# Starting eight expert tiles while the last batches are still routed

## The reference, cut to what matters

```
x = x + attention(layernorm(x))          # linear attention with a 5-tap convolution of v, gated
x = x + moe(layernorm(x))                # 8 experts, the 2 best of each token
moe: p = softmax(y @ gate_w.T); for each token the two experts with the largest p
     h = silu(y @ w1[e] + b1[e]);  out += p[e] * (h @ w2[e] + b2[e])     # 128 -> 512 -> 128
```

## Time and profile before

| | us |
|---|---|
| median of 3 runs | 636.82 |
| the runs | 631.85 to 644.96 |
| the profiled execution, own time | 633.09 |
| its span, first to last instruction | 631.3 |
| PE busy | 538.6 (85%) |
| DVE busy | 464.5 (74%) |
| POOL busy | 373.4 (59%) |
| ACT busy | 295.6 (47%) |
| mean granted TensorE clock | 0.919 of 2.4 GHz |

### The profile page before, as it was taken

How to read it: one execution, slowest core, us unless ns; L and a number is a source line. 1 busy time by engine, 2 the same in 40 slices (tenths; PEclk the granted TensorE clock), 3 DMA queues, 4 the chain that set the end, 5 groups by cost and what they waited for, 6 DMA issues and landing times.

```text
span 631.3 us, 10741 instructions
## 1 busy us (share of the span) xinstructions
PE 538.6 (85%) x2977; PEld 430.6 (68%) x2977; DVE 464.5 (74%) x1391; ACT 295.6 (47%) x658; POOL 373.4 (59%) x318
## 2 busy tenths in 40 slices
PE   3999999999999999996302999999899999999970
PEld 2787777777877777775202888877677777877750
DVE  6567868888788888865451888886887788878860
ACT  2434423333233333312301677765776676767750
POOL 3333266677666777766760000178848888888885
PEclk9899979999899999985555999999999999999995
DMA  8415787775767741111138476788889999999844
GB/s 294 130 66 160 291 284 250 261 255 186 261 232 261 262 158 34 36 37 35 50 138 290 159 263 238 256 267 264 249 280 300 279 275 304 306 288 309 276 123 97
DMA packets 66827, 134.23 MB, mean 213 GB/s; under 512 B 8144, under 2 KB 26704, under 8 KB 61648
## 3 DMA queue, kind: packets, MB, share of 16 engines
q1 hardware_dynamic: 51408, 116.23, 52.1%
q0 software_dynamic: 15360, 17.32, 12.5%
HBM read 29.83 MB, written 62.54 MB: 146 GB/s over the span
## 4 chain that ended last, share of the span: by engine, by line
PE 63%; DVE 10%; issue 10%; POOL 5%; DMA 5%; ACT 2%; SPq 2%; POOLq 1%; another core or an unknown queue 1%; DVEq 0%; ACTq 0%
PE conv L419 5%; PE qp L483 5%; PE qp L421 4%; PE qp L482 4%; PE qp L419 4%; PE conv L420 4%; PE conv L421 4%; PE rows L414 4%; PE qp L420 4%; POOL xres L759 3%; PE kv L443 3%; PE kvp L419 3%; PE kvp L421 3%; PE kvp L420 3%; PE gate_wo L471 2%
## 5 line engine op out<-in xcount | busy, mean ns | idle before, releaser
L718 POOL DMA_INDIRECT rows_in<-yrow,slots x128 | 124.4, 972 | 55.4 <-issue 35.0
L755 POOL DMA_INDIRECT got<-rows_out,slots x64 | 68.0, 1062 | 102.8 <-issue 102.5
L759 POOL DMA_INDIRECT xres<-rows_out,slots x64 | 103.2, 1612 | 19.5 <-issue 19.2
L1065 DVE TENSOR_TENSOR hl<-hf,hh 128x512 fp32r<-128x512 f32 x156 | 108.8, 698 | 5.4
L1063 DVE CAST hh<-hf 128x512 fp32r<-128x512 f32 x156 | 71.4, 458 | 37.2 <-ACT hf L688 33.1
L688 ACT ACTIVATE hf<-qp,wst 128x512 f32<-128x512 f32 x104 | 72.3, 695 | 47.7 <-PE qp L421 31.9
L613 ACT ACTIVATE yrow<-xres,nb,rs 128x128 f32<-128x128 f32 x64 | 26.4, 482 | 54.1 <-DVE nb L933 49.7
L688 ACT ACTIVATE hf<-kvp,wst 128x512 f32<-128x512 f32 x52 | 36.1, 695 | 26.9 <-PE kvp L421 13.3
L419 PE MATMUL qp<-xT_h,wst 128*128 128x512 f32 x104 | 45.6, 438 | 2.0 <-DVE xT_l L1033 1.6
L740 POOL TENSOR_TENSOR rs<-ve,half 128x8 f32<-128x8 f32 x20 | 35.9, 1795 | 18.6 <-DVE ve L810 17.2
L674 ACT ACTIVATE yo<-gate_wo,wv 128x128 f32<-128x128 f32 x156 | 44.2, 373 | 0.9 <-PE gate_wo L414 0.7
(11 more groups left out here) (182 smaller groups left out, 1480.3 us busy)
## 6 DMA issues: line engine op xcount, KB each, us to landing
wst<-wres SPq DMA_DIRECT2D x39, 1030.5 KB
rows_out<-tail SPq DMA_DIRECT2D x28, 1280.0 KB
xg<-rows_in SPq DMA_DIRECT2D x39, 272.0 KB
rows_out<-yo SPq DMA_DIRECT2D x39, 256.0 KB
wraw<-in_w_experts SPq DMA_DIRECT2D x8, 512.0 KB, 4.2
out_x<-xres SPq DMA_DIRECT2D x16, 256.0 KB
rows_in<-tail SPq DMA_DIRECT2D x9, 272.0 KB, 4.2
rows_in<-yrow,slots POOLq DMA_INDIRECT x128
```

Of the source, the lines that this page charges most:

```text
L718: nc.gpsimd.indirect_dma_start(rows_in, bass.IndirectOffsetOnAxis(ap=slots[:, f, k, j:j + 1], axis=0), rows_of(f)[:, j, :], None).then_inc ...
L755: nc.gpsimd.indirect_dma_start(got[b % N_GOT][:, j, :], None, rows_out, bass.IndirectOffsetOnAxis(ap=slots[:, b, 1, j:j + 1], axis=0)).the ...
L759: nc.gpsimd.indirect_dma_start(xres[:, b * SUB + j, :], None, rows_out, bass.IndirectOffsetOnAxis(ap=slots[:, b, 0, j:j + 1], axis=0), com ...
L1065: nc.vector.tensor_tensor(hl[c][:], hf[c][:], hh[c][:].bitcast(F32), ALU.subtract).then_inc(s["h_low"], 1)
```

## The change

The expert stage no longer waits for the last batches. Names are those of the changed kernel.

- **Early table.** After eight batches (EARLY_FROM = 8) there are at least eight full pages (N_EARLY = 8). In steps 13, 14 and 15 of the attention stage PE and DVE build a small table of the eight full pages that were touched first (`trow_e`, `texp_e`), each part at the end of the DVE's step. It uses free columns of the PSUM bank of `kv`, so PE's `kv` matmuls of steps 14, 15 and 16 wait for the DVE's part before them.
- **Early start.** The attention loop ends after step 16 (NB + 1). SP loads the weights and rows of tile 0 once the attention's last uses of that memory are past, and PE starts tile 0 after `oT` of the last batch. DVE first finishes the choice of batch 13.
- **Drain in pieces.** What steps 17 to 20 and the table did is cut up and stands in `drain(t, c)` behind chunk c of tile t, on PE, ACT and DVE, from tile 0 to tile 5. ACT's exponentials of batches 14 and 15 stand between silus.
- **Table and tails.** SP writes the zero rows behind the lists ahead of its work for tile 6 (LAST_LOAD: before it loads the rows of tile 7 and the weights of tile 6), and waits for the full table and all scatters ahead of its work for tile 7 (TABLE_AT).
- **The way back.** `got` is now the memory of `yrow`, of which there are five instead of six, so N_GOT is 5: gather(b) waits for the add of batch b-5. A batch is added behind the tile of this rule: at least max(2(b+1)+7, 16) + 6, and at most one batch a tile. That gives tiles 22, 23, 24, 25, 26, 27, 28, 29, 31, 33 and so on to 45 for batches 0, 1, 2 ... 15.
- **Buffers.** The tiles' transposes have a PSUM bank of their own (XT), the banks of the `down` sums go from three to two, `xT_h` and `xT_l` from three to two, `hf`, `hh` and `hl` from four to three. The constants are loaded in two more transfers.

```diff
-N_GOT = 4
-LEAD, LAG = 2, 5
-N_YROW = 6
+N_H = DOWN_LAG + 1
+N_XT = 2
+LEAD = 2
+N_YROW = 5
+N_GOT = N_YROW
+N_EARLY = E
+EARLY_FROM = -(-(E * (TS - 1) + (N_EARLY - 1) * TS + 1) // (TOP_K * S))
+LAST_LOAD, TABLE_AT = N_EARLY - 2, N_EARLY - 1
...
+        got = [r[:, :, 0:D] for r in yrow]
...
-        HB, YB, TY = [qp[:, 0:512], qp[:, 512:1024], kvp[:, 0:512]], [kvp[:, 512:1024], KV[:], CV[:]], GW
+        HB, YB, TY, XT = [qp[:, 0:512], qp[:, 512:1024], kvp[:, 0:512]], [kvp[:, 512:1024], KV[:]], GW, CV
...
         def tiles_until(b):
-            return min(TOP_K * (b + 1) + E - 1, N_TILES)
+            return min(max(TOP_K * (b + 1) + E - 1, N_EARLY + E), N_TILES)
+        add_at = []
+        for b in range(NB):
+            add_at.append(max([tiles_until(b) + ADD_LAG + 1] + [t + 1 for t in add_at[-1:]]))
+        def added(t):
+            return add_at.index(t) if t in add_at else None
...
         @block.sync
...
-            sp.wait_ge(s["fill_ready"], 1)
-            for e in range(E):
-                r = sp.value_load(fill_at[0:1, e:e + 1], min_val=e * CAP, max_val=e * CAP + N_TOK)
-                sp.dma_start(rows_in[bass.ds(r, TS), :].rearrange("(p j) w -> p j w", p=P), tail[:]).then_inc(s["tails_in"], 16)
-            sp.wait_ge(s["table_ready"], 3)
+            def fill_ends():      # the same wait and loop
...
+            sp.wait_ge(s["clear_in"], N_CLEAR * 16)
+            sp.wait_ge(s["table_e"], 2)
+            scattered(EARLY_FROM)
+            for name in ("conv_psum", "k_sin", "vtok_ready", "ks_masked", "q_rot"):
+                sp.wait_ge(s[name], NB)
             load_weights(0)
...
             load_rows(0)
             for t in range(LAST_STEP + 1):
+                if t == LAST_LOAD:
+                    fill_ends()
+                if t == TABLE_AT:
+                    sp.wait_ge(s["table_ready"], 3)
+                    sp.wait_ge(s["tails_in"], E * 16)
+                    sp.wait_ge(s["dummy_in"], 16)
+                    scattered(NB)
                 if real(t + 1):
                     load_rows(t + 1)
                 if real(t) and t > 0:
                     load_weights(t)
...
         @block.tensor, step(i, par)
+                    after(pe, "touch_e", 1 if i == NB - 2 else 0)
+                    after(pe, "pos_e", 1 if i == NB - 1 else 0)
+                    after(pe, "table_e", 2 if i == NB else 0)
                     for j in range(SUB):
                         last = nc.tensor.matmul(KV[:, 0:D + 1], ktok[:, j, :], vtok[:, j, :],
...
-            for i in range(-LEAD, NB + LAG):
+            for i in range(-LEAD, NB + 1):
                 step(i, i % 2)
+            def drain(t, c):
+                if (t, c) == (0, 0):
+                    rank(NB - 3)
+                if (t, c) == (0, 2):
+                    leave_attention(NB - 1)
+                if (t, c) == (0, 3):
+                    rows_to_gate(NB - 2)
+                if (t, c) == (1, 0):
+                    gate(NB - 2)
+                if (t, c) == (2, 0):
+                    rank(NB - 2)
+                if (t, c) == (2, 3):
+                    rows_to_gate(NB - 1)
+                if (t, c) == (3, 0):
+                    gate(NB - 1)
+                if (t, c) == (4, 0):
+                    rank(NB - 1)
+                if (t, c) == (4, 2):
...                                        # slots_ready 16, then the matmul for cum_psum
+                if (t, c) == (5, 0):
...                                        # diag_ready, then two matmuls for touch_psum
+                if (t, c) == (5, 2):
...                                        # pick_ready, need_ready, then two matmuls for table_psum
-            pe.wait_ge(s["table_ready"], 3)
+            pe.wait_ge(s["o_ready"], NB)
             rows_to_features(0)
...
         @block.scalar
+            def drain(t, c):               # called behind chunk c, but not in chunk 2
+                if (t, c) == (0, 1):
+                    rows_normal(NB - 2)
+                if (t, c) == (0, 3):
+                    save_rows(NB - 2)
+                if (t, c) == (1, 0):
+                    save_logits(NB - 2)
+                if (t, c) == (1, 1):
+                    exponents(NB - 2)
...                                        # the same for NB - 1 at (2, 1), (2, 3), (3, 0), (3, 1)
         @block.gpsimd, gather(b)
+                if b < N_GOT:
+                    after(pool, f"scat{b}", fills(NB - 1 - b, N_YROW) * (SUB * TOP_K * 16), alone=True)
                 after(pool, "combined", b - N_GOT + 1, alone=True)
...
         @block.vector
+            def early_table(i):            # at the end of step(i)
+                if i == NB - 3:
...
+                    counts(early[:, 0:EARLY_FROM * E].rearrange("p (b e) -> p b e", b=EARLY_FROM), EARLY_FROM)
+                    link(nc.vector.tensor_scalar(valid[:], cum[:, EARLY_FROM - 1:EARLY_FROM], entry_from, float(TS),
+                                                 ALU.subtract, ALU.is_ge))
+                    link(nc.vector.tensor_tensor(n_touched[:], n_touched[:], valid[:], ALU.mult))
+                    nc.vector.scalar_tensor_tensor(key[:], n_touched[:], float(RE), entry_no, ALU.mult, ALU.subtract)
+                    nc.vector.tensor_scalar(diag16[:], idn, n_touched[:], None, ALU.mult).then_inc(s["touch_e"], 1)
+                if i == NB - 2:
+                    dve.wait_ge(s["key_psum_e"], 1)
+                    order(early)
+                    nc.vector.tensor_scalar(rest[:], pos[:], float(N_EARLY), None, ALU.is_lt).then_inc(s["pos_e"], 1)
...
+                if i == NB - 1:
...                                        # two small operations into trow_e and texp_e, table_e
+            def drain(t, c):
+                if (t, c) == (0, 0):
+                    shifts(NB + 1)
+                    place(NB - 3)
+                if (t, c) == (0, 2):
+                    residual(NB - 1)
+                if (t, c) == (0, 3):
...                                        # four bn_stats
+                if (t, c) == (1, 0):
...                                        # four bn_aggr
+                    variances(NB + 1, (NB + 1) % 2)
+                    shift_logits(NB - 2)
+                if (t, c) == (1, 2):
+                    choose_first(NB - 2)
+                if (t, c) == (1, 3):
+                    choose_second(NB - 2)
+                if (t, c) == (2, 0):
+                    shifts(NB + 2)
+                    place(NB - 2)
...                                        # batch NB - 1: logits (3, 0), choice (3, 2), (3, 3), place (4, 0)
+                if (t, c) == (4, 2):
+                    table_counts()
+                if (t, c) == (5, 0):
+                    table_order()
+                if (t, c) == (5, 2):
+                    table_rows()
...
             for t in range(LAST_STEP):
                 for c in range(FC if real(t) else 0):
...
+                    drain(t, c)
-                if second_add(t) is not None:
-                    add(second_add(t))
+                if added(t) is not None:
+                    add(added(t))
```

More of the change, by code:

```diff
@@ L70, with build @@
 X_GROUPS = ((0, 1), (1, 2), (2, 4), (4, 8), (8, 12), (12, 16))
-def build(nc, x, first, second, tables_k, table, w_experts, b_experts, out):
+def build(nc, x, first, w_proj, second, late, tables_k, table, w_experts, b_experts, out):
     rows_in = nc.dram_tensor("rows_in", (DUMP * TS + TS, ROW), F32, kind="Internal").ap()
@@ L114, in build @@
         table_load = sb("table_load", [1, 1])
+        oT = sb("oT", [P, S])
+        yT = sb("yT", [P, S])
+        yrow = [sb(f"yrow{i}", [P, SUB, ROW]) for i in range(N_YROW)]
+        got = [r[:, :, 0:D] for r in yrow]
         tail = sb("tail", [P, TSUB, ROW])
@@ L170, in sa @@
             return attention.enter_context(nc.sbuf_tensor(name, shape, dt))
+        wraw = [sa(f"wraw{i}", [P, WPACK]) for i in range(2)]
         second_sb = sa("second_sb", [P, sum(SECOND.values())])
@@ L402, in _ @@
                     store_rows(t - NBUF)
-                if second_add(t - 2) is not None:
-                    leave(second_add(t - 2))
+                if added(t - 2) is not None:
+                    leave(added(t - 2))
             for k in range(NBUF):
@@ L428, in project, with rank @@
                         True, True).then_inc(s[name], 1)
+            def rank(f):
+                after(pe, "oh_ready", f + 1)
+                after(pe, "xnTl_ready", all_of(f + 5))
+                after(pe, "lgs_ready", all_of(f + 1))
+                for j in range(SUB):
+                    dst = XB[:, j * E:(j + 1) * E]
+                    last = nc.tensor.matmul(dst, bef16[:], oh16[:, j, :], start=True, stop=(f == 0 and j == 0))
+                    for k in range(j):
+                        last = nc.tensor.matmul(dst, one16[:], oh16[:, k, :], start=False, stop=(f == 0 and k == j - 1))
+                    if f > 0:
```

(36 more changed lines are left out.)

372 lines of the change are left out of this document (214 added, 158 removed).

## The result

The changed kernel takes 653.81 us (median of 4 runs, 652.09 to 656.46), the kernel before 634.34 us (4 runs). The ratio is 1.031, 95% interval 1.025 to 1.038; on a second chip it was 1.030 (1.021 to 1.039). The forecast was 641 with a range of 625 to 657, and "no change" as the likeliest. The measured time is in the range and on the forecast's side. But it is outside the 2% that I had called no change: forecast were some 4 us of loss over the 636.82 then known, measured are 19.5. The range held by its width.

A forecast was written before the change was run, and what follows sets the result against it. POOL, fully booked from batch 5, was taken to set the end: start 302.1 + D 28 + 157.7 to batch 0's add + 150.8 for fetches and tail, less 1, gave a span of 637.6; 641 us was named, range 625 to 657.

The forecast's parts named there:

- no change: Whole kernel: measured time within about 2%, 624 to 650 us; chance 0.62.
- What sets the end: POOL from batch 5: fetch waits for batch 0's add near 488, some 20 us idle, then no hole to the end.
- D: Delay of the drained tiles: 13 + 3.4 + 8.7 + 3 = 28 us, between 13 and 38.
- The start: Tile 0's first `up` at 302.1, 41.6 us earlier, including 4.6 us of `kv` waiting for DVE.
- DVE becomes the bound there: First six tiles: 20.3 us of drain work on DVE against 7.2 free, 13 us more.
- the switches: ACT's table changes between silu and exponential and back, twice, in tiles 1 and 3: 3.4 us in all (0 to 5.6).
- The waits for weights: DVE waits 8.7 us (0 to 13) for tile 6's weights behind SP's writes, then 3 us (0 to 5) behind the table.
- rival (b), the clock: Drained tiles: PE's clock stays at 1.2 GHz, a tile takes about 12 us, 12 us more over five, 651; chance 0.2.
- a clock of 0.50 beyond tile 1: Sign for PE in the tiles: the forecast is wrong if its clock is 0.50 beyond tile 1.
- idle time of DVE in the drained tiles: Sign on DVE: no idle time was expected in tiles 1 and 3 to 5, but about 9 us before `wsel` in tile 5.
- slower: Whole kernel: slower than the 624 to 650 of no change; chance 0.26, of which 0.15 from the clock rival.

The follow-up runs named there:

- e1: Changed kernel with the late adds undone (adds behind tiles 15, 17, 19 ... as before); ratio 1.004 to the kernel before, span 628.9.
- e5: Kernel before with only the changed one's late adds and five got buffers, no early start or drain; ratio 1.034 to the kernel before, span 645.8.
- e7: e6 with ranks and places of batches 14 and 15 and the table's parts one chunk later on PE and DVE; 610.51 us, ratio 0.987 to the kernel before.
- e6: e4 with SP asking for tile 7's weights before its wait for table and writes; 613.85 us, ratio 0.988 to the kernel before.
- e8: e7 with ACT's exponentials of batches 14 and 15 replaced by copies, so another choice of experts; ratio 0.979 to the kernel before.
- e2: Changed kernel with the eight writes behind the lists issued by POOL after its last scatter, not by SP; ratio 1.024 to the kernel before, span 634.9.
- e4: Changed kernel with adds by the old rule and the writes behind the lists on POOL; 616.28 us, ratio 0.991 to the kernel before.

## Why the prediction was right, and where it was not

**What sets the end: right.** The forecast counted along POOL: add of batch 0 behind tile 22, eleven batches and a tail. Predicted were a hole of some 20 us before batch 5, no hole after it, and 149.8 us from there to the end; measured 23.70, none, and 148.9. Only the fetch itself came at 504.39 and not near 488, which is the term D below. e1 and e5 show it from both sides. PE's last tile is done long before: the transposes of tile 38 stand at 606.63, 46.7 us before the end, against 32.7 before.

**The start: right.** Predicted 302.1, measured 301.0 (304.95 on the second chip, 305.48 in e1, with the same code there). `kv` waited 2.91 us in step 14 and 1.55 in step 15, as the early table wanted (PE's timeline):

```profile
247.48 2.06 PE L525 MATMUL kv<-vtok,ktok 128*128 128x129 f32 x8 [2.91 <-DVE diag L1149]
267.62 1.13 PE L525 MATMUL kv<-vtok,ktok 128*128 128x129 f32 x8 [1.55 <-DVE rest L1153]
```

**The step that failed: the delay D of the drained tiles.** I had 28 us, with 38 as the upper bound. From the start of tile 0 to the end of batch 0's add it was 202.6 us instead of 157.7, so D was 44.9. This one term, 16.9 too small, is the whole difference between 637.6 and 653.3 (start -1.1, POOL's tail and its release -0.1).

Not all of the 44.9 comes with the change each time. In the second profile of the same kernel that stretch is 185.9 us (304.95 to 490.89). That makes D 28.2 by the 157.7 of the first chip, and 33.9 by the same count in the kernel before on its own chip (483.81 + 5.66 - 337.39 = 152.1). So the forecast missed D by up to 17 us in one execution and by 6 at most in the other. The ratio is 1.03 all the same, because there tile 0 starts only 32.4 us earlier than in the kernel before (337.39), not 42.7.

The windows from the first transposes of tile 1 to those of tile 6, and from there to tile 8, tell what was wrong with it (changed kernel, then e1, then e7 with its own tiles 1, 6 and 8):

```profile
304.29:361.38 57.09, 45.74 (x220) 35.48 (x219) 40.39 (x132) 32.51 (x63) 24.07 (x24) 0.81 0.37 130
361.38:392.99 31.61, 19.97 (x67) 14.32 (x66) 14.83 (x37) 10.92 (x24) 1.47 (x2) 0.69 0.61 219
```

```profile
308.76:360.74 51.98, 43.65 (x220) 34.12 (x219) 40.45 (x134) 32.89 (x64) 23.57 (x22) 0.84 0.41 146
360.74:387.22 26.48, 16.66 (x67) 11.89 (x66) 13.94 (x35) 10.13 (x21) 2.88 (x3) 0.81 0.67 240
```

```profile
304.54:351.86 47.32, 40.97 (x218) 31.80 (x217) 38.52 (x127) 33.08 (x65) 19.89 (x19) 0.94 0.48 172
351.86:371.63 19.77, 16.55 (x69) 12.72 (x68) 15.80 (x41) 9.83 (x21) 10.74 (x14) 0.83 0.64 232
```

- *"DVE becomes the bound there": wrong as it ran.* In the five tiles DVE is busy 40.39 of 57.09 us, 71%, less than in a steady tile, and I had foreseen no idle time on it. No engine is booked. What I had summed, 20.3 us of work against 7.2 free, would give 13 and with the switches 16.4; the five tiles lost 57.1 - 5 x 6.45 = 24.8 us (19.7 in e1 and in the second profile, with the same code there). The work of the drain is a chain from engine to engine, and each link blocks what is written behind it on its engine. DVE's waits from 290 to 380 are led by silus that ACT had not yet done (us in total, times, longest):

```profile
DVE hh L1267 <- ACT hf L796: 13.1, 8, 3.5
DVE wsel L1245 <- DMA wst<-wres: 8.2, 1, 8.2
```

  How the 24.8 divide is shown only in part. e7, with PE's waits for `oh` all but gone, takes 5.6 us less than e6, and e8, without the switches, 4.8 less than e7. What is left in e8 is 42.5 us with DVE busy for 38.26 of them, 90%:

```profile
307.32:349.82 42.50, 39.47 (x218) 30.96 (x217) 38.26 (x127) 27.87 (x61) 20.75 (x19) 0.97 0.55 192
```

  So DVE does come near to being the bound once the waits are taken away, and 10.3 us over five steady tiles then remain, near my 13. The waits come on top of that, and beyond the 3.4 for the switches the sum had no term for them in these tiles.

- *The waits for weights: right in size, wrong in what follows.* I had 8.7 and 3, measured are 8.22 and 2.80. But the two tiles lost 31.6 - 12.9 = 18.7 us. From 370 to 380, in the wait, PE was busy 4.18 us of 10 and the granted clock 0.50, which is 1.2 GHz, and what followed began at that level (0.50 from 380 to 382, with PE busy all the time): PE was busy 19.97 us in these two tiles with work for 13. That is rival (b), the clock, which I had given a chance of its own instead of a place in the sum; it came in part, in tiles 6 and 7 and from 344 to 353, and not over five tiles. By two signs that I had named, a clock of 0.50 beyond tile 1 and idle time of DVE in the drained tiles, this part of the prediction is wrong.

The page TensorE: Matmul & The Clock Gate of the Trainium skill (The HAM clock gate) has the clock fall with PE's idleness and rise with work; the trace agrees at 370 to 380 (0.50) and at 450 to 500 (1.00).

Not settled: with the same code there, tiles 1 to 8 take 95.5 us in the changed kernel's first profile, 84.9 in e1 and 85.3 in its second profile. A part is SP's eight writes, 11.97, 10.27 and 8.74 us, and a stall of ACT in the first, 2.31 us before `lgs`, for which the trace names no releaser. The first profile, on which the numbers above rest, has some 10 us that the other two do not.

**"No change" had 0.62, "slower" 0.26.** With the upper bound of 38 for D the sum gives a span of 647.6, 2.6% over. The outcome slower was within my own bounds, and the even spread around 28 hid it.

**Why 42.7 us of an earlier start came to nothing.** In e1, without the late adds, tile 0 starts some 38 us before (305.48), and batch 4 is fetched at 465.74, 1.5 us before. Tiles 1 to 8 took 84.9 us where they took 51.9 before, so 33 of the 38 us were spent there. In the mended e7 batch 4 is fetched at 447.05. That is 20 us before, but those are of a slower chip; in the second profile of the kernel before, on a chip where it takes 618 us as it takes 619 on e7's, batch 4 comes at 456.99. The 10 us between them fit the 8.7 us by which e7 is under the kernel before.

## What to carry to other kernels

When one engine is booked without a hole to the end, cost a change by when that engine's unbroken run begins, not by when the stage begins. Look for who hands it its buffers: here one line on where the adds stand in DVE's order cost 3%, more than the early start of a whole stage brought in the best version (1.3%). Work cut up and put between the chunks of another loop was not paid by busy time against free time alone: its pieces that cross engines cost waits on top (24.8 us in five tiles, where busy time gave 16.4), and the stall that let TensorE's clock fall to 1.2 GHz was paid a second time in the matmuls behind it (20 us for work of 13). And take a second profile before one term is blamed: here two of the same kernel differ by 10 us in eight tiles.

## What the runs showed of the hardware

The address loads and issues of eight transfers from SP took 10.58 us in the hole between the stages, 11.97, 10.27 and 8.74 among the tiles (changed kernel, e1, changed kernel again). The same eight from POOL took 6.1 us, from 360.30 to 366.36, in e2. POOL's rate for the fetches hardly differed from run to run: over its unbroken run, from batch 5 to the end of the last fetch's issue, a batch takes 13.2 us in the kernel before (both profiles) and 13.0 to 13.3 in the changed one (both profiles), e1, e4 and e7.
